# A chain of convolutions and mixed matrices: the first convolution goes ahead of the sixteen matrix sets

## The reference

```python
x = x + conv(x, L0_weight) + (cond @ L0_c_weight.T)[:, :, None] + fside[None, :, None]
x = x + einsum('boi,bih->boh', agg_w1, x) + agg_b1[:, :, None]
x = x + conv(x, L2_weight) + (cond @ L2_c_weight.T)[:, :, None] + fside[None, :, None]
x = x + einsum('boi,bih->boh', agg_w3, x) + agg_b3[:, :, None]
```

## Time and profile before

| | |
|---|---|
| median of 3 runs | 2476.03 us |
| the profiled execution, its own time | 2476.58 us |
| its span | 2474.8 us |
| busy | PE 99%, DVE 86%, ACT 61%, POOL 1% |
| first convolution starts | 37.04 us |
| first mixing starts | 54.57 us |

### The profile page before, as it was taken

The page is one execution under the profiler, slowest core; times in us unless marked ns, Lnnn a source line. Parts: engine busy times, 40 slices in busy tenths (PEclk is TensorE's granted clock), DMA queues, the critical chain, the costliest instruction groups (busy, mean ns, idle before and its releaser), DMA issues.

```text
span 2474.8 us, 99123 instructions
## 1 busy us (share of the span) xinstructions
PE 2456.0 (99%) x45256; PEld 1472.7 (60%) x45256; DVE 2117.3 (86%) x806; ACT 1519.9 (61%) x1120; POOL 23.3 (1%) x28
## 2 busy tenths in 40 slices
PE   8999999999999999999999999999999999999998
PEld 4444444455555555566666666666666666666665
DVE  7988988988988889889889888898898898888984
ACT  6666666666666656666666666666666666666665
POOL 3000000000000000000000000000000000000000
PEclk9999999999999999999999999999999999999999
DMA  9644444444444444444444444444444444444433
GB/s 348 208 128 127 157 140 127 141 151 132 127 145 152 127 127 158 138 127 143 150 131 127 146 150 127 129 157 138 127 144 150 130 127 149 148 127 129 159 104 121
DMA packets 186683, 357.24 MB, mean 144 GB/s; under 512 B 12754, under 2 KB 143834, under 8 KB 154010
## 3 DMA queue, kind: packets, MB, share of 16 engines
q1 hardware_dynamic: 186056, 354.60, 45.8%
q10 hardware_dynamic: 594, 2.13, 0.2%
HBM read 205.69 MB, written 150.99 MB: 144 GB/s over the span
## 4 chain that ended last, share of the span: by engine, by line
PE 98%; DVE 1%; ACT 1%; DMA 0%; issue 0%; SPq 0%; DVEq 0%; ACTq 0%
PE psum L410 62%; PE psum L481 35%; PE psum L379 0%; DMA out<-outb 0%; DMA diff<-expert_rows 0%; ACT shared L629 0%; DVE diff L759 0%; ACT diff L629 0%; DVE y L797 0%; DVE y L813 0%; DVE y L816 0%; ACT y L657 0%; ACT outb L680 0%; DVE h L789 0%; ACT y L629 0%
## 5 line engine op out<-in xcount | busy, mean ns | idle before, releaser
L410 PE MATMUL psum<-diff,prod_w 32*64 32x512 f32 x28672 | 1689.2, 587 | 2.2 <-issue 1.0
L410 PEld LDWEIGHTS psum<-diff,prod_w 32*64 32x64 f32 x28672 | 952.4, 131 | 629.7 <-issue 304.9
L754 DVE TENSOR_TENSOR diff<-xin 128x2052 f32<-128x2052 f32 x256 | 975.9, 3903 | 307.5 <-PE psum L410 307.5
L481 PE MATMUL psum<-y,mixw 32*64 32x512 f32 x16384 | 1028.7, 588 | 1.9 <-DVE y L816 1.9
L481 PEld LDWEIGHTS psum<-y,mixw 32*64 32x64 f32 x16384 | 575.3, 131 | 341.7 <-issue 186.5
L754 DVE TENSOR_TENSOR diff<-x 128x2055 f32<-128x2055 f32 x255 | 568.7, 2301 | 0.0
L720 ACT ACTIVATE x<-psum,bias_now 128x2048 f32<-128x2048 f32 x128 | 251.7, 1966 | 198.3 <-PE psum L481 198.3
L680 ACT ACTIVATE outb<-psum,bias_now 128x2048 f32<-128x2048 f32 x128 | 251.0, 1961 | 195.3 <-PE psum L481 193.8
L645 ACT COPY shared<-psum 128x2048 f32<-128x2048 f32 x128 | 238.8, 1866 | 171.8 <-PE psum L410 171.8
L838 DVE TENSOR_TENSOR y<-y,shared 128x2048 f32<-128x2048 f32 x126 | 288.7, 2291 | 15.6 <-ACT y L659 15.6
L673 ACT COPY y<-psum 128x2048 f32<-128x2048 f32 x126 | 235.6, 1870 | 91.8 <-PE psum L410 91.8
(11 more groups left out here) (80 smaller groups left out, 104.2 us busy)
## 6 DMA issues: line engine op xcount, KB each, us to landing
xin<-x SPq DMA_DIRECT2D x128, 1024.0 KB, 7.0
out<-outb SPq DMA_DIRECT2D x127, 1024.0 KB, 4.8
mixw<-mix_dram SPq DMA_DIRECT2D x512, 128.0 KB, 5.4
mix_dram<-shared SPq DMA_DIRECT2D x6, 1024.0 KB, 12.9
mix_dram<-y SPq DMA_DIRECT2D x6, 1024.0 KB, 10.7
mix_dram<-diff SPq DMA_DIRECT2D x2, 1024.0 KB, 12.0
mix_dram<-outb SPq DMA_DIRECT2D x2, 1024.0 KB, 13.9
y<-experts ACTq DMA_DIRECT2D x2, 512.0 KB, 4.3
```

The lines of the kernel that those rows point to most:

```text
L410: return pe.matmul(psum[cols, half, g, :], prod_w[v][at, kind, s, cols], moving, start=start, stop=stop, skip_group_check=True)
L481: mm = pe.matmul(psum[cols, half, r, :], mixw[home][at, b, g, cols], y[home][at, :, g, b, :], start=g == 0, stop=g == GROUPS - 1)
L754: nc.vector.tensor_tensor(into(kind), in0, in1, op).then_inc(diff_ready[v], 1)
```

## The change

The first convolution (pair 0) comes first and all sixteen sets after it (`make_matrices`); the first mixing follows, with the bias products inside it. ACT sorts x of pair 0 into phases in x2, so that three of its four differences are made by DVE from sorted data; the first sum is made in two pieces, one for each sample. GpSimd blends the bias of the experts and makes the first convolution's outputs. Experts are loaded by SP instead of ACT, behind the taps and x. The homes are given out anew: sets 0, 1 and then 3, 4 in x2, 2, 5, 6, 7 in diff0, 8, 9 in rows[0], 10, 11 in shared[1], 12, 13 in y[1], 14, 15 in outb. Every set is now halved between ACT and DVE. Sets of layer 1 are stored in two parts, first the rows of samples 0 and 1 and then the other 126. The core of the diff:

```diff
+        FIRST_IN_X2, IN_DIFF0, IN_ROWS, IN_SHARED, IN_Y, IN_OUT = (0, 1), (2, 5, 6, 7), (8, 9), (10, 11), (12, 13), (14, 15)
+        THEN_IN_X2 = (3, 4)
+        PICKED_OUT = 3
...
+            def store_picked(j):
+                sp.wait_ge(*taken(j))
+                sp.wait_ge(*upper_taken(j))
+                sp.dma_start(columns_of(0, j)[0:PB], homes[j][0:PB]).then_inc(agg_stored[j], 16)
...
+                rest = slice(PB if m == 0 else 0, B)
+                sp.dma_start(columns_of(m, part)[rest], homes[j][rest]).then_inc(agg_stored[j], 16)
+
+            load_taps(0)
+            load_x_on(sp, 0)
+            for m in range(2):
+                sp.dma_start(expert_sb[m], experts[m]).then_inc(experts_loaded[m], 16)
+            load_rows(0)
+            load_rows(1)
+            load_taps(1)
+            sp.wait_ge(diff_ready[0], 1)
+            sp.wait_ge(x_sorted, PB)
+            load_x_on(sp, 1)
+            for j in range(PICKED_OUT):
+                store_picked(j)
                 store_agg(j)
-            load_taps(1)
+            for j in range(PICKED_OUT, SETS):
+                store_picked(j)
             sp.wait_ge(taps_ready, 1)
             for j in range(SETS):
-                sp.wait_ge(agg_stored[j], 16)
+                sp.wait_ge(agg_stored[j], 32 if j < PICKED_OUT else 16)
             load_mix_on(sp, 0, 0)
-            sp.wait_ge(diff_ready[0], PRODUCTS)
-            load_x_on(sp, 1)
-            for j in range(SETS, AHEAD):
+            for j in range(PICKED_OUT, 2 * SETS):
                 store_agg(j)
...
+            pool.wait_ge(att_ready, 1)
+            pool.wait_ge(through_taken, 1)
+            done(pool.tensor_tensor(weighted[0], weighted[0],
+                                    hid[0]["att"][:, :, 0:1].to_broadcast([P, EXPERTS, P]), ALU.mult))
+            blend_experts(0)
...
+            pool.wait_ge(shared_ready[0], COPIES)
+            pool.wait_ge(sums_taken[0], 2)
+            pool.tensor_tensor(flat[:, 0], flat[:, 0], kept[:, 1], ALU.subtract).then_inc(y_ready[0], 1)
...
+            pool.tensor_tensor(flat[:, 1], flat[:, 1], kept[:, 0], ALU.add).then_inc(y_ready[0], 1)
+            pool.wait_ge(scaled, 1)
+            blend_experts(1)
...
+            for j in THEN_IN_X2:
+                pool.wait_ge(*stored(j))
+            clear_gaps()
...
+            def make_matrices():
+                turn_attention()
+                pe.wait_ge(sums_taken[0], 2)
+                bias_through_experts(1, B_HALF)
+                pe.wait_ge(att_t_ready, 2)
+                pe.wait_ge(rows_loaded[0], 16 * 2)
+                pe.wait_ge(sums_taken[0], 3)
+                aggregate(0, 0, half_of(0))
+                pe.wait_ge(scaled, 1)
+                aggregate(0, 1, half_of(1))
+                for j in range(2, 2 * SETS):
+                    if j == SETS:
+                        pe.wait_ge(rows_loaded[1], 16 * 2)
+                    pe.wait_ge(*taken(j - 2))
                     pe.wait_ge(*upper_taken(j - 2))
+                    aggregate(j // SETS, j % SETS, half_of(j))
...
-                    mix(0, 0, (agg_part, 1), taken(AHEAD), taken(AHEAD + 1), nothing, parts=True)
+                    last = 2 * SETS - 2
+                    mix(0, 0, taken(last), upper_taken(last), (bias_ready, 2), finish_biases)
...
             def take_agg(j):
                 act.wait_ge(agg_pe, j + 1)
+                if j in THEN_IN_X2:
+                    act.wait_ge(*stored(j - 3))
+                if j == IN_Y[1]:
+                    act.wait_ge(blended, 2)
+                nc.scalar.copy(homes[j][:, 0:2], psum[:, half_of(j), 0:2, :]).then_inc(agg_taken["act"], 1)
...
+            for j in range(2 * SETS):
                 dve.wait_ge(agg_pe, j + 1)
-                nc.vector.tensor_copy(homes[home_of[j]][:, PH // 2:PH], psum[:, half_of(j), PH // 2:PH, :]
+                if j in THEN_IN_X2:
+                    dve.wait_ge(*stored(j - 3))
+                if j == IN_Y[1]:
+                    dve.wait_ge(blended, 2)
+                nc.vector.tensor_copy(homes[j][:, PH // 2:PH], psum[:, half_of(j), PH // 2:PH, :]
                                       ).then_inc(agg_taken["dve"], 1)
...
                 if whole(i) and i == 0:
-                    dve.wait_ge(conv_done[0], CONV_SIGNALS)
-                    diff_of_xin(1, (BOTH, SIGNED, ONLY_EVEN, ONLY_ODD))
+                    for j, kind in zip(IN_DIFF0, PROD_ORDER):
+                        dve.wait_ge(*stored(j))
+                        diff_of_xin(1, (kind,))
```

More of the change, by code:

```diff
@@ L76, in conditioned_layers @@
         rows = [diff2[:].rearrange("p n c -> p (n c)")[:, 0:SLICE], outb[:].rearrange("p b l -> p (b l)")]
[L77 to L80, removed]
+        blend = y[1][:].rearrange("p j g b r -> p (j g b r)").rearrange("p (n c) -> p n c", n=4)
@@ L81, in conditioned_layers @@
+        expert_sb = [blend[:, m].rearrange("p (k o) -> p k o", k=EXPERTS) for m in range(2)]
+        weighted = [blend[:, 2 + m].rearrange("p (k o) -> p k o", k=EXPERTS) for m in range(2)]
         centre_taps = [mixw[v][:].rearrange("p b g o -> p (b g o)")[:, 0:BANK].rearrange("p (s c) -> p s c", s=PH)
                        for v in range(2)]
[L83 to L91, removed]
+        FIRST_IN_X2, IN_DIFF0, IN_ROWS, IN_SHARED, IN_Y, IN_OUT = (0, 1), (2, 5, 6, 7), (8, 9), (10, 11), (12, 13), (14, 15)
+        THEN_IN_X2 = (3, 4)
+        FULL = PH * BANK
+        homes = {}
@@ new lines, in conditioned_layers @@
+        for n in range(2):
+            homes[FIRST_IN_X2[n]] = homes[THEN_IN_X2[n]] = x2[:, n * FULL:(n + 1) * FULL]
+            homes[IN_ROWS[n]] = rows[0][:, n * FULL:(n + 1) * FULL]
+            homes[IN_SHARED[n]] = shared[1][:, n].rearrange("p g c -> p (g c)")
+            homes[IN_Y[n]] = y[1][:, n].rearrange("p g b r -> p (g b r)")
+            homes[IN_OUT[n]] = outb[:, n, :]
+        for n in range(PRODUCTS):
+            homes[IN_DIFF0[n]] = diff0[:, n, 0:FULL]
+        homes = {j: h.rearrange("p (r c) -> p r c", r=PH) for j, h in homes.items()}
@@ L424, in divided_set, with conv @@
                 return mm
-            def conv(v, n, a_free, b_free, diffs, late, halves=(A, B_HALF), second=nothing, odd=None):
+            def conv(v, n, a_free, b_free, diffs, late, halves=(A, B_HALF), second=nothing, odd=None, first=False):
                 A, B_HALF = halves
                 sem_a, count_a = a_free
-                pe.wait_ge(taps_ready, v + 1)
+                if not first:
+                    pe.wait_ge(taps_ready, v + 1)
                 pe.wait_ge(diff_ready[v], diffs[0])
@@ L652, in take_sums @@
                 nc.scalar.copy(shared[v][:, 1, 2:4], psum[:, B_HALF, 2:4, :]).then_inc(shared_ready[v], 1)
-                if whole(n) and n == 0:
-                    for j in LAST_IN_Y[v]:
-                        act.wait_ge(agg_stored[j], 16)
+                if whole(n) and n == 0 and v == 1:
+                    for j in IN_Y:
+                        act.wait_ge(*stored(j))
                 act.wait_ge(conv_done[v], done + 5)
```

295 lines of the change are left out of this document (148 added, 147 removed).

## The result

The changed kernel takes 2503.8 us (median of 5 runs, 2500.8 to 2505.55) against 2476.03 (5 runs, 2475.29 to 2476.53): a ratio of 1.0109 (95% interval 1.0098 to 1.0121), 27.8 us slower. The profiled execution took 2503.8, its span is 2502.0. The forecast was 2489.3 with a range of 2480.5 to 2496: the direction was right, the size was half. All ratios compare runs of the faster state; one run of the kernel with a further small store, 4386.6 us, is left out of its ratio.

A forecast was written before the change was run, and what follows sets the result against it. Bounds: PE, 99% busy, and a second chain without slack through stores, x(2) and differences to the third x convolution. Profiled 2476.58 + 13.3 = 2489.9; the median, 0.55 lower, gave 2489.3, range 2480.5 to 2496.

The forecast's parts named there:

- The chain: Stores, x(2), three differences, then the third x convolution at 108.3 instead of 95.02: 13.3 us late.
- PE's own mixing: Mixing that would start near 89 waits for pair 1's matrix until some 97 and ends at 104.
- The start: First convolution starts at 15.0 instead of 37.04: experts land at 12.9, then their product takes 1.98.
- the clock: Slow clock after PE's gap between about 8 and 12.9: 1.7 us charged, lower bound 0.
- Sets 3 and 4: They wait for the stores of sets 0 and 1, done at 39.8 and 42.4; set 4 out at 43.6.
- The stream of thirteen stores: Remaining stores issued from 52.2, 13 x 2.6 = 33.8 plus 3.5 for filling and landing: last lands at 89.5.
- The rival of uneven stores: A 126-row store takes 2.93 instead of 2.6: 1.9 us more, 2491.2 in all; chance 0.28.
- the small store: Set 7's small store, ahead of pair 0's loads, lands at 49.7: 2.2 us taken, bounds 1.5 and 3.4.
- the lone store: A 1 MB store alone, releasing set 3's home, takes about 5 us; lower bound 4.5.
- x(2) behind the last store: x(2), queued behind the stores, takes 7.5 us and is whole at 97.0; bounds 5.2 and 8.8.
- The PE chain alone: First mixing starts near 56.6 instead of 54.57; by this chain alone the kernel loses 1 to 2 us.
- GpSimd was hidden: Beside the first convolution and sets: two outputs of 5.1 us each end near 40, second blend by 43.

The follow-up runs named there:

- the kernel with a further small store: Kernel before, whole stores, plus one 2-row store to an unread tensor ahead of each of sets 0 to 7: 2479.7 us, ratio 1.0013.
- taking the bytes away: Changed kernel's order, 18 or 16 rows stored per set instead of 128, all pairs mixed with pair 0's matrices: 2477.1 us, ratio 1.0001.
- two stores less ahead of x(2): Changed kernel with the stores of sets 14 and 15 issued behind x(2) and pair 1's matrices: 2497.1 us, ratio 1.0088.
- the kernel with new homes: Changed kernel, samples 0 and 1 also stored to their own tensor, whole stores, sets 3, 4 in shared[1], 10, 11 in shared[0]: 2493.6 us, ratio 1.0068.
- Even pieces: Changed kernel with layer 1 sets stored as 16 then 112 rows, instead of 2 then 126: 2500.8 us, ratio 1.0097.
- the changed one with whole stores: Changed kernel without small first stores, each set stored whole when made, pair 0's matrices loaded behind the first eight: 2491.2 us, ratio 1.0057.
- two kernels before with cut stores: Kernel before, sets 0 to 7 stored as 2+126, 16+112 or 64+64 rows: 2483.0, 2480.8, 2479.1 us; which two is not stated.

## Why the prediction was right in kind and wrong in size

- **The chain** stores, x(2), three differences, third x convolution was right: a shift of PE at 122.81 accounts for the whole difference, taking the bytes away takes all of it away, and two stores less ahead of x(2) give 6.1 back. But the last link was close: PE's own mixing, forecast to end at 104, waited for the matrices of pair 1 until 113.16 and ended 0.5 before the difference came. Both chains stand behind the same stores.
- **The start** was 16.85, not 15.0. Experts landed near the 12.9 I took; the product ran at half clock (3.78 instead of 1.98). I had charged the clock once, 1.7, which is about what it cost; the term was placed too late and the experts' landing a little early.
- **Sets 3 and 4** waited as forecast, but the stores of sets 0 and 1 let DVE go on at 41.9 and 45.7, not 39.8 and 42.4: the second lone store came 3.8 behind the first, not 2.6. The clock fell behind the waits (0.50 in 45 to 50, where the kernel with new homes, which has no such waits, shows 1.00), so sets 5 to 7 took 1.7 to 2.4 us each instead of 1.28. I had not priced that. Together the thirteen stores started 4.3 late (56.5 for 52.2), and the first mixing 4.9 late (61.5 for 56.6).
- **The stream of thirteen stores** is the step that failed: 46.8 us from first issue to last landing instead of 37.3, 9.5 of the 14.5 us by which the third x convolution was missed. I took the rate of the kernel before, 403 GB/s, for stores of another shape and order. At 126 rows it was 322, and 391 in 80 to 85 behind them. From 56.5 to 103.3 the mean was 341 GB/s, 16.0 MB, which is 2.4 MB more than the thirteen stores: the loads of pair 0 and part of x(2) and of the loads behind it moved there as well. At 403 GB/s 16.0 MB take 39.7 us, so by this estimate some 7 of the 9.5 us are the rate and the rest is bytes that I had not counted there. The rival of uneven stores priced a part (9/8, 1.9 us). My bounds moved the start, the clock, the small store, the x and the lone store, but never these 13 x 2.6, the largest term. Even pieces made x(2) whole 4.1 earlier (107.3), an estimated 1.5 of it by fewer bytes held back. Why the rate is low at a full share is open.
- **The rest** of the 14.5 is the late start of these stores (4.3, above) and 0.6 for x(2).
- **x(2) behind the last store** took 8.1, taken as 7.5; the three differences took 11.4, taken as 11.2. Both held.
- **The PE chain alone** was forecast to lose 1 to 2 us; without the bytes it lost 0.5, within the interval. GpSimd was hidden, as forecast: its outputs took 4.5 each and ended at 39.2.

The Trainium skill's rule on the number of engines of a transfer (DMA: Bandwidth & Descriptors, "Why a DMA increments its semaphore by 16 and not by 1") gives 14 of 16 for 126 rows, 0.875. The traces agree: 14/16 of the 1.03 to 1.05 of whole stores is 0.90 to 0.92, and 126 rows show 0.90 to 0.91. The rule alone does not give the rate: 14/16 of 403 GB/s is 353, and 318 to 328 was measured in the kernel before with 126 rows.

## What to carry to other kernels

Before moving transfers from beside one piece of work to behind it, add up the bytes behind the last early point and divide by the rate of the same shape: here 13 stores, x(2) and the mixing loads, 17 MB at 320 to 390 GB/s, outlast every compute step up to the third convolution. A buffer refilled behind such a stream carries its whole length to the engine that reads it. Holding bulk back to let a small urgent transfer pass only moves the debt: held back, x(2) was late; not held back, the first matrices were.

## What the runs showed of the hardware

- A second queue did not carry small transfers past a full one: four loads of 128 KB took 8.2 us from ACT's queue beside SP's stores, and 2.8 to 3.1 from SP's where no bulk stood ahead of them.
- A transfer more costs even if it is small: eight further DMAs of 16 KB ahead of the stores, 3.2 us (0.7 to 5.7 by the interval).
- Whole stores ran at 399 to 408 GB/s in the kernel before (20 to 35 us) and at 378 to 381 in the changed one with whole stores (40 to 55 us), with the same shapes. The chip is not the reason: on the chip of the latter, two kernels before with cut stores moved their whole ones at 404 and 400 (58 to 70 us). Why is open.
- ACT sorted 128x2048 from SBUF into phases in 3.96 us; from the accumulators into a like pattern it takes 1.97. Source and pattern both differ, so which of them costs is open.
